# Three-part bf16 side taps in the first convolution, weights quantised by GpSimd, columns by VectorE

## The reference

```python
# L0: attention over the 1024 pixels of each image
scores = einsum('bci,bcj->bij', c_, b_)          # c_, b_, d_: 1x1 convolutions of x
A = softmax(scores, axis=1)
e = x + alpha * einsum('bcj,bkj->bck', d_, A)
x = conv1x1(e, wd1, bd1) + conv1x1(e, wd2, bd2)
# L1: two 3x3 convolutions with 3-bit weights, batch norm of this batch
out = relu(batchnorm(conv3x3(x, lsq_quantize(w1, alpha1)), gamma1, beta1))
out = batchnorm(conv3x3(out, lsq_quantize(w2, alpha2)), gamma2, beta2)
x = relu(out + x)
# L2: two 3x3 convolutions with 4-bit weights (tanh, divided by its largest value), fixed norm
# L3: 1x1 convolution to 16 channels, batch norm, box filter, batch norm
h = box_conv(relu(bn(einsum('oc,bchw->bohw', w1, x))), x_min, x_max, y_min, y_max)
x = relu(x + bn(h))
```

## Time and profile before

| what | us |
|---|---|
| median of 3 runs | 157.21 (157.13 to 157.22) |
| profiled execution, its own time | 158.21 |
| its span, first to last instruction | 156.4 |
| TensorE busy | 140.5 (90% of the span) |
| VectorE busy | 117.5 (75%) |
| ScalarE busy | 83.8 (54%) |
| GpSimd busy | 51.6 (33%) |
| mean granted TensorE clock | 0.980 of full speed |

### The profile page before, as it was taken

One profiled execution on the slowest core, in us unless ns is written; L12 is line 12 of the kernel. 1 busy time (PEld: TensorE's weight loads), 2 busy tenths in 40 slices (PEclk: granted clock), 3 DMA queues, 4 the chain that ended last, 5 costly groups with the idle time before them and its releaser, 6 DMA issues.

```text
span 156.4 us, 2621 instructions
## 1 busy us (share of the span) xinstructions
PE 140.5 (90%) x945; PEld 65.9 (42%) x945; DVE 117.5 (75%) x280; ACT 83.8 (54%) x138; POOL 51.6 (33%) x97
## 2 busy tenths in 40 slices
PE   7989999999999999999999997999979996989600
PEld 2244422333323432333345854786357632378500
DVE  2189989899878789999912667787788569875882
ACT  3135566356766777467815105995192537533282
POOL 7018999999910006000000950000066000000080
PEclk9999999999999999999999999999999999999975
DMA  3586020200002000000000000001000000000015
GB/s 101 133 293 272 4 66 3 67 2 0 0 6 67 0 0 0 0 0 4 0 0 0 0 0 2 4 0 38 0 0 0 4 0 0 0 6 4 0 67 201
DMA packets 2748, 5.27 MB, mean 34 GB/s; under 512 B 368, under 2 KB 1200, under 8 KB 2608
## 3 DMA queue, kind: packets, MB, share of 16 engines
q1 hardware_dynamic: 2592, 4.98, 10.3%
q10 hardware_dynamic: 144, 0.13, 0.3%
HBM read 3.13 MB, written 1.05 MB: 27 GB/s over the span
## 4 chain that ended last, share of the span: by engine, by line
PE 69%; DVE 15%; ACT 6%; issue 5%; DMA 2%; ACTq 0%; DVEq 0%
PE ps L420 16%; PE ps L412 15%; PE ps L476 13%; PE ps L493 7%; DVE nmax L1006 3%; PE ps L490 3%; PE ps L352 3%; PE ps L639 3%; DMA wbc<-wa 2%; ACT box_t L685 2%; DVE dz L896 2%; PE ps L648 2%; DVE tmpo L1119 1%; PE ps L380 1%; PE ps L362 1%
## 5 line engine op out<-in xcount | busy, mean ns | idle before, releaser
L685 ACT ACTIVATE probs<-ps,nmax 128x1024 f32<-128x1024 f32 x32 | 35.6, 1114 | 25.9 <-DVE nmax L1006 25.9
L1006 DVE TENSOR_REDUCE nmax<-ps 128x1 f32<-128x1024 f32 x32 | 39.0, 1220 | 4.8 <-PE ps L412 4.5
L420 PE MATMUL ps<-probs,dz 128*64 128x512 f32 x128 | 31.4, 606 | 0.0
L412 PE MATMUL ps<-xd,g 64*128 64x512 f32 x48 | 24.0, 616 | 0.4 <-ACT probs L685 0.4
L412 PE MATMUL ps<-xd,g_other 64*128 64x512 f32 x48 | 24.0, 616 | 0.0
L420 PEld LDWEIGHTS ps<-probs,dz 128*64 128x64 f32 x128 | 7.6, 136 | 20.6 <-issue 16.9
L476 PE MATMUL ps<-img,wq 128*128 128x512 f32 x48 | 13.6, 422 | 1.0 <-ACT img L685 0.8
L1323 POOL TENSOR_TENSOR box_t<-box_t 128x256 f32<-128x256 f32 x8 | 6.1, 797 | 24.1 <-issue 24.1
L1290 POOL TENSOR_TENSOR box_t<-parm,consts 128x256 f32<-128x256 f32 x24 | 13.9, 617 | 0.0
L903 DVE TENSOR_TENSOR img<-y,img 128x512 fp32r<-128x512 f32 x11 | 7.6, 690 | 8.1 <-ACT y L685 8.1
L896 DVE TENSOR_SCALAR dz<-d,rz 128x64 f32<-128x64 f32 x32 | 12.2, 381 | 1.1
(11 more groups left out here) (177 smaller groups left out, 242.7 us busy)
## 6 DMA issues: line engine op xcount, KB each, us to landing
wraw<-wconv SPq DMA_DIRECT2D x1, 1152.0 KB, 7.8
xd<-x SPq DMA_DIRECT2D x4, 256.0 KB, 4.7
g_other<-g SPq DMA_DIRECT2D x6, 128.0 KB, 2.3
out<-box_t SPq DMA_DIRECT2D x3, 256.0 KB, 2.5
consts<-cst SPq DMA_DIRECT2D x1, 327.0 KB, 4.2
out<-box_t SPq DMA_DIRECT2D x2, 128.0 KB, 2.2
wdd<-wa SPq DMA_DIRECT2D x1, 192.0 KB, 2.4
parm<-par SPq DMA_DIRECT2D x1, 163.0 KB, 2.5
```

The source lines that it names most:

```text
L412: last = mm(o[:, 512 * p:512 * p + 512], rows, cols, start=True, stop=True)
L420: last = mm(y[64 * p:64 * p + 64, :], dz[:, g % DZ, :], probs[:, g % PROBS, 512 * p:512 * p + 512], start=g == 0, stop=t == JT - 1)
L685: return nc.scalar.activation(o, i, f, **kw)
L1006: V.tensor_reduce(nmax[:, i:i + 1], slot(("S", i)), AX.X, ALU.min).then_inc(max_ready, 1)
```

## The change

Three things are done.

First, the side taps of the first convolution. The input gets three bf16 parts: the image rounded (`thirds[0]`, into img3), the rest rounded (`thirds[1]`), and what then remains (`thirds[2]`, both in the new img0). ScalarE makes the first two (`first_third` at tiles 13, 21, 29, `second_third` at 15, 23, 31, and both at the end for image 3). VectorE makes the differences (`rest_of` at 14, 22, 30; `last_third` at 17, 25; the others behind the last tile). The side taps become 72 matmuls of 64 x 64, in fours, and need no wait where rows are changed. The main taps stay as they are.

Second, GpSimd quantises all four weights: the first two behind the edges (`quantised`), the last two behind `wden`, which VectorE computes at tile 26 now. The weights get tiles of their own, and the odd images of the second convolution read w1x, a copy of w1c with the halves crossed, which SyncE transfers.

Third, the columns are subtracted by VectorE, behind the low parts of the second convolution, in four pieces. GpSimd clears img3 and img0 at the start.

```diff
-            for i, last_tap in ((odd, o), (even, e)):
...
+            def side_taps0(even, odd, begin=(), stop=()):
+                top, low = slice(0, 64), slice(64, 128)
+                for part in range(3):
+                    pe.wait_ge(thirds[part], odd + 1)
+                    for a in range(3):
+                        for to_even in (True, False):
+                            for b in (even, odd):
+                                q = low if to_even else top
+                                o = top if to_even == (b == even) else low
+                                last = mm(ps[o, BANKS[0][b], :], w0s[q, a, :],
+                                          image0(part, b, a, -1 if to_even else 1, q),
+                                          start=b in begin and part == a == 0, stop=b in stop and part == a == 2)
...
+            def finish0():
+                side_taps0(0, 1, stop=(0, 1))
+                side_taps0(2, 3, begin=(3,), stop=(2,))
+                main_taps(0, 3, 0, begin=False)
+                main_taps(0, 3, 1, begin=False, stop=True)
...
+            def first_third(b):
+                act.wait_ge(img3_zero, 2)
+                act.wait_ge(gen[0], b + 1)
+                run(image0(0, b), as_rows(y1[:, b, :]), ACT.Copy).then_inc(thirds[0], 1)
+            def second_third(b):
+                act.wait_ge(rest_done, b + 1)
+                run(image0(1, b), as_rows(rest[:, b % 2, :]), ACT.Copy).then_inc(thirds[1], 1)
...
+            def rest_of(b):
+                dve.wait_ge(thirds[0], b + 1)
+                V.tensor_tensor(as_rows(rest[:, b % 2, :]), as_rows(y1[:, b, :]), image0(0, b), ALU.subtract)\
+                    .then_inc(rest_done, 1)
+            def last_third(b):
+                dve.wait_ge(thirds[1], b + 1)
+                V.tensor_tensor(image0(2, b), as_rows(rest[:, b % 2, :]), image0(1, b), ALU.subtract)\
+                    .then_inc(thirds[2], 1)
...
-                if i == 24:
-                    lsq_clip(0)
...
+                if i in (14, 22, 30):
+                    rest_of((i - 14) // 8)
+                if i in (17, 25):
+                    last_third((i - 17) // 8)
...
-            lsq_clip(1)
-            lsq_round(1)
-            lsq_main(1)
-            lsq_side(1)
+            rest_of(NB - 1)
+            last_third(NB - 1)
...
-            tanh_weights(2)
-            tanh_weights(3)
+            dve.wait_ge(edge_clip, 4 * PIECES)
+            for i in range(4):
+                n = slice(512 * i, 512 * i + 512)
+                V.tensor_tensor(edge_buf[3][:, n], edge_buf[2][:, n], edge_buf[3][:, n], ALU.subtract)\
+                    .then_inc(cols_ready, 1)
...
+            G.memset(img3[:], 0.0).then_inc(img3_zero, 1)
+            G.memset(img0[:], 0.0).then_inc(img3_zero, 1)
...
+            def quantised(k):
+                pool.wait_ge(wconv_in, 16)
+                pool.wait_ge(lsq_done, 1)
+                w = wtmp[:, k, :]
+                link(G.tensor_scalar(w, wraw[:, k, :], lsq_r[:, k:k + 1], QP, ALU.mult, ALU.min))
+                link(G.tensor_scalar(w, w, QN, MAGIC, ALU.max, ALU.add))
...
+            quantised(0)
+            quantised(1)
             pool.wait_ge(wmax_part, 2)
             G.partition_all_reduce(wmax_all[:], wmax[:], 128, bass.bass_isa.ReduceOp.max).then_inc(wmax_done, 1)
...
-            pool.wait_ge(lo_done, NB)
-            pool.wait_ge(edge_clip, 4 * PIECES)
-            for hi, lo in zip(pieces(edge_buf[2]), pieces(edge_buf[3])):
-                G.tensor_tensor(lo, hi, lo, ALU.subtract).then_inc(cols_ready, 1)
+            tanh_weights(2)
+            tanh_weights(3)
```

More of the change, by code:

```diff
@@ L215, in image, with image0 @@
             return img[q, part, b, first:first + H * PITCH].rearrange("q (r s) -> q r s", s=PITCH)[:, :, 0:S2]
+        def image0(part, b, kh=1, ds=0, q=slice(0, 128)):
+            first = 1 + PITCH * kh + ds
+            of_part = img3[q, b] if part == 0 else img0[q, part - 1, b]
+            return of_part[:, first:first + H * PITCH].rearrange("q (r s) -> q r s", s=PITCH)[:, :, 0:S2]
         def image3(b, kh=1, ds=0, q=slice(0, 128)):
@@ L244, in build @@
         hi_own, lo_own = sem("hi_own"), sem("lo_own")
+        thirds = sems("third", 3)
+        rest_done, lsq_done, wden_done, w1x_in = (sem(n) for n in ("rest_done", "lsq_done", "wden_done", "w1x_in"))
         conv_done = sems("conv_done", 4)
@@ L300, in _ @@
                                  g32[64 - 64 * half:128 - 64 * half, b - 1, :]).then_inc(g_in[b - 1], 16)
+            sp.wait_ge(wq_ready[1], 3)
+            for half in range(2):
+                sp.dma_start(w1x[64 * half:64 * half + 64].bitcast(F32), w1c[64 - 64 * half:128 - 64 * half].bitcast(F32)).then_inc(w1x_in, 16)
             sp.wait_ge(wq_ready[3], 4)
@@ L480, in main_taps @@
                     last.then_inc(conv_done[k], 1)
[L482 to L494 removed]
+            def side_taps0(even, odd, begin=(), stop=()):
[10 more added lines that the diff above has]
+                                          start=b in begin and part == a == 0, stop=b in stop and part == a == 2)
+                                if part == a == 2 and not to_even and b in stop:
+                                    last.then_inc(conv_done[0], 1)
@@ new lines, in side_taps1 @@
+            def side_taps1(even, odd, to_even, begin=(), stop=()):
+                top, low = slice(0, 64), slice(64, 128)
+                for part in range(2):
+                    for a in range(3):
+                        for b in (even, odd):
+                            q = low if to_even == (b == even) else top
+                            end = part == 1 and a == 2
+                            last = mm(ps[:, BANKS[1][b], :], (w1c, w1x)[b % 2][q, 3 + a, :],
+                                      image(part, b, a, -1 if to_even else 1, q),
+                                      start=b in begin and part == a == 0, stop=end and b in stop)
+                            if end:
+                                last.then_inc(conv_done[1] if b in stop else sides_done, 1)
@@ new lines, in side_taps2 @@
+            def side_taps2(even, odd, begin=False, stop=()):
+                for part in range(2):
+                    for a in range(2):
+                        end = part == a == 1
+                        o = mm(ps[:, BANKS[0][odd], :], w2[64:128, 3 + a, 64 * (odd % 2):64 * (odd % 2) + 128],
+                               image(part, odd, a + 1, -1, slice(64, 128)),
+                               start=begin and part == a == 0, stop=end and odd in stop)
+                        e = mm(ps[:, BANKS[0][even], :], w2[0:64, 3 + a, 64 * (even % 2):64 * (even % 2) + 128],
+                               image(part, even, a, 1, slice(0, 64)), start=False, stop=end and even in stop)
@@ L580, in _ @@
             convolve(1, 2)
-            finish(1)
+            finish1()
             average(1)
```

194 lines of the change are left out of this document (100 added, 94 removed).

## The result

The changed kernel takes 157.08 us in the median of 22 runs (154.77 to 157.68), the kernel before 157.14 us beside it; the ratio is 0.993, with a 95% interval of 0.990 to 0.996. The forecast, 157.9 us and slower, was wrong: the kernel isn't slower. The ratio, 0.7% faster, leaves out runs over 1.5% above their kernel's fastest, which are 11 of the changed kernel's 22, while the medians take all runs and show no difference (0.06 us). So how much faster it is depends on the measure, because its runs spread more: its lowest is 1.7 us under the lowest of the kernel before (156.48), while its upper half lies where that kernel's does. That spread is half of this study.

What follows compares the result with a forecast made beforehand. TensorE bounds attention, so its waits there are lost; the first convolution's side taps are on the path behind. Terms: -1.65 side taps, +0.10 columns, +2.2 attention = +0.65 us, 157.21 to 157.9 us, range 156.0 to 159.3.

Steps and rivals of the forecast that it cites:

- Side taps: First convolution behind attention: 18 groups of four matmuls take 4.58 us instead of 6.23, gaining 1.65 us; the split hides.
- rival E: Only two quadrants run together in the side taps: 9.0 us, 4.4 more than forecast, 162.3 us; chance 0.02.
- Columns: VectorE's four subtractions delay ScalarE's masked copies past the second normalisation's square root, costing 0.10 us.
- Step 1: Attention, score tile 17: rest_of(0) and the edge clip ahead of a maximum make TensorE lose 0.25 to 0.6 us.
- Step 2: Attention, tiles 20 and 21: VectorE waits for GpSimd's weight instructions; with step 1, TensorE loses 1.4 to 2.95 us.
- Steps 3 and 4: Later attention: GpSimd's second stint (weights 3 and 4) and ScalarE's six copies cost no loss.
- Rival D: Start: VectorE's copy of b3 may wait for GpSimd's long memset, delaying b: +1.0 us, 158.9 us; chance 0.05.
- rival A: GpSimd's instructions are shorter or enter only in VectorE's pauses; step 1 alone stays: 156.1 us, faster; chance 0.30.
- rival B: Short end of GpSimd's instruction lengths: loss 1.2 to 1.85 us, 156.9 to 157.5 us, no difference; chance 0.22.

Runs made afterwards that it cites:

- no_parts: borders without the split's second and third parts, the first convolution's side taps reading the first part three times; 155.94 us (12 runs).
- again: The changed kernel unaltered, run again; 156.87 us (12 runs) against 157.12 of the kernel before.
- pairs: The changed kernel with GpSimd's clip and rounding of weights 1 and 2 each made a multiplication and an addition; 156.86 us (10 runs).
- start_pieces: The changed kernel with its one clearing of img0 on GpSimd cut into eight of 580 columns; 156.35 us (6 runs).
- borders: The changed kernel with GpSimd clearing only the borders of img3 and img0 that no copy writes; 155.88 us (11 runs) against 157.00 of the kernel before.
- borders_2: borders unaltered, run again on one chip with no_parts and after_2; 156.25 us (11 runs) against 156.80 of the kernel before.
- no_stint: The changed kernel without GpSimd's clip and rounding of weights 1 and 2, their outputs made behind the reduction; 157.05 us (10 runs).
- after_2: The changed kernel unaltered, on the same chip as borders_2; 157.50 us (12 runs) against 156.80 of the kernel before.
- blocked: The changed kernel with GpSimd waiting for the first weights' landing before it clears img0; 157.20 us (6 runs), ratio 1.002 to the kernel before.

## Why the prediction was wrong, point by point

**Side taps: right, gain undersized.** -1.98 instead of -1.65 us. The four matmuls of a group run together, which disposes of rival E. The term took 0.25 for a group and 0.33 for the last from the earlier trace rows, eight matmuls long; over 72 it is 0.236 for each. Every one of the sixteen traces repeats it: 24.07 to 24.18 us from the first side tap to bn_std, against 26.08 and 26.02 with the old ones. The split is ready as forecast (last part from 87.14, forecast 87.0).

**Columns: +0.10 forecast, none measured.** The four subtractions stood 0.60 us apart, not 0.705: of the four in the forecast's row one took 1.10 us and the others 0.68. So the copies ended 0.2 us ahead of the root instead of 0.09 behind it, and the wait that the forecast named wasn't the last one. The margin is thin: in no_parts, where they ended last, the root came 0.08 us later (24.18 instead of 24.10).

**Step 1, tile 17: the row right, the sum wrong.** `rest_of(0)` took 0.94 us beside the edge clips, 0.25 over its usual 0.69, and TensorE stood 0.39 us ahead of tile 17 in that execution: within 0.25 to 0.6. But the stall of 0.36 ahead of tile 13, which the kernel before has, was gone; attention was no longer. In again the one at tile 13 is there and the one at 17 is not. What was taken for an addition was an exchange in these two, but not a rule: `pairs` and start_pieces have both, with an attention of 74.56 and 74.19 us, and borders and borders_2 have neither, with 73.62 and 73.53. So such a stall is worth about 0.3 us, and whether it falls differs between executions of like code.

**Step 2, tiles 20 and 21: this step failed.** The forecast had 0.8 to 2.35 us for it; no stall stands there. The maxima of tiles 18 and 19 start at 49.82 and 51.32, as before, where the forecast had them 1.8 us or more later. Two of its links broke. The lengths of GpSimd's instructions were read from rows with other operators: 0.8 to 1.3 us forecast for 576 columns, 2.1 to 2.8 measured; only the output forms, with one operator, came near the forecast's upper end (0.69 us for 192 columns against 0.67, 1.18 for 384 against 1.33). The stint ends at 59.5, not at 51 to 54. And the rule "VectorE waits till GpSimd's ends", read from rows of GpSimd's edge additions and an instruction beside them, was carried to others: beside the long ones VectorE mostly had its usual lengths, and where `dz` was held, the maximum behind it went ahead in its time. What settles it is no_stint: without clip and rounding the attention is the same (73.83 and 73.89 us). `pairs`, which has about the forecast's short lengths, shows the second link alone: `dz` at 0.40 to 0.55, and behind the start of its edit one stall of 0.35 us, which the changed kernel has too, not the forecast's 1.4.

**Steps 3 and 4: right.** No stall behind 57 us in any of the sixteen traces, and no cost of ScalarE's copies is seen.

**Rival D: right mechanism, wrong weight.** It got 0.05 on the condition that the weights land 0.15 us later than 4.55. In after_2 the copy was held with a start of 4.58, 0.03 later. `blocked`, where by its edit every run should be held, has its lowest at 156.83 and its median at 157.20; of the changed kernel's 46 runs 29 lie above 156.7, of borders' 23 three. The start of one trace was taken for the start of all. The price of +1.0 was about right where TensorE's first products are short: it waits 0.84 to 1.21 us for b then, and nothing where they are long. Without the clearing the median is 1.2 us lower.

**The sum.** -1.98 + 0 + 0 is what the profiled executions show (-1.80 with start and end); from 157.21 that gives 155.2. The lowest runs of the two kernels do lie 1.55 to 1.71 us apart in the three sets. But borders, the changed kernel less its long clearings, has medians of 155.88 and 156.25, only 1.1 and 0.55 us under the kernel before beside it; what takes the rest isn't shown. So its closeness to rival A's 156.1 is partly luck: A has a gain 0.33 too small and 0.50 of costs that the profiled executions don't show. The changed kernel's 157.08 is near A plus the price of D, and it also lies in rival B's range, 156.9 to 157.5; that too is luck, since neither B's short instructions nor its loss at tiles 20 and 21 is there.

## What to carry to other kernels

An engine that comes to stand beside another costs time by what is held behind it on the path: look whether the next instruction that TensorE waits for needs the held one at all. Read a GpSimd duration only from a row with the same operators and the same kind of operands. And a margin of 0.1 us against a transfer's landing is none: a long clearing that isn't urgent has to end before the first transfer lands, be cut down to the borders, or wait until the instruction beside it is through (blocked waited only for the landing, and met the copy), since its cost shows in some executions and not in the one that was profiled.

## What the runs showed of the hardware

On GpSimd, 576 fp32 columns cost 0.7 us with multiply and add and 2.1 to 2.8 with multiply and minimum or maximum and add. The Trainium skill ("GPSIMD Engine Reference", "Engine selection") calls one-input work there roughly line-rate; `pairs` agrees roughly, with 1.2 to 1.3 ns a column where VectorE's form in the earlier trace rows has 0.94; the mixed pairs at 3.7 to 4.8 don't, and neither does the subtraction with one operator, at 3.1 to 3.6 (1.18 us for 384 columns, 0.69 for 192).

TensorE's first eight fp32 products took between 2.1 and 4.0 us in different executions, with the granted clock shown as 1.00 in all. The first four took 1.07 to 1.97 us, the second four 1.13 to 2.08. In the four traces with 2.08 TensorE had idled for 0.59 to 0.68 us ahead of the first; after 0.57 us in borders they took 1.52 and 1.13. What decides it isn't shown; a slower clock that the rows don't show isn't ruled out. By itself it moves the start by up to 1.8 us.
